# Node numbers of a compare read from PSUM, and two edge tiles instead of one fetched by one-hot products in every second step of the maximum rounds

## The reference: what is computed

```
# L0, one "sum" round: every node sums its neighbours' scaled rows
m_j = norm[:, None] * x[from_]
out = segment_sum(m_j, to_, num_segments=n)

# L3, three "max" rounds (l = 0, 1, 2)
xi = x[dst]
xj = x[src]
h = relu(concat([xi, xj - xi]) @ W1[l] + b1[l])
out = segment_max(h @ W2[l] + b2[l], dst, num_segments=n)
x = relu(where(isfinite(out), out, 0.0))
```

## Time and profile before

| | before |
|---|---|
| median of 3 runs | 8224.27 us (8218.69 to 8224.7) |
| the profiled execution | 8205.95 us, span 8204.1 us |
| busy share | POOL 76%, PE 54%, DVE 47%, PEld 41%, ACT 20% |
| mean granted TensorE clock | 0.686 of full speed |

### The profile page before, as it was taken

One profiled execution on the slowest core, in us unless ns is written; L12 is line 12 of the kernel. 1 busy time (PEld: TensorE's weight loads), 2 busy tenths in 40 slices (PEclk: granted clock), 3 DMA queues, 4 the chain that ended last, 5 costly groups with the idle time before them and its releaser, 6 DMA issues. The chain is left out here.

```text
span 8204.1 us, 96536 instructions
## 1 busy us (share of the span) xinstructions
PE 4466.8 (54%) x27562; PEld 3368.7 (41%) x27562; DVE 3884.1 (47%) x5429; ACT 1605.5 (20%) x2960; POOL 6273.6 (76%) x5477
## 2 busy tenths in 40 slices
PE   2444445665666656621112566666566666666665
PEld 2334334555565555411111344444344444344443
DVE  6555555666646666512212444444444443444444
ACT  0000002333323333300000111121111111111111
POOL 6888886777767777567777788888788887788887
PEclk8667665666656666755555677777677777677776
DMA  7555555777757777622222344443444443444443
GB/s 153 135 134 132 131 129 109 147 147 148 145 116 145 147 146 148 136 72 58 59 58 57 86 96 94 96 95 88 93 95 97 95 95 87 93 96 95 96 96 77
DMA packets 2168031, 886.49 MB, mean 108 GB/s; under 512 B 1794743, under 2 KB 2044260, under 8 KB 2161108
## 3 DMA queue, kind: packets, MB, share of 16 engines
q1 hardware_dynamic: 1083012, 446.95, 23.8%
q10 hardware_dynamic: 909808, 252.48, 13.5%
q0 software_dynamic: 174688, 180.89, 12.0%
HBM read 610.50 MB, written 269.09 MB: 107 GB/s over the span
## 5 line engine op out<-in xcount | busy, mean ns | idle before, releaser
L1183 POOL DMA_INDIRECT edges_a<-src_table,idx x3643 | 4546.7, 1248 | 1265.9 <-issue 1098.8
L1190 POOL DMA_INDIRECT edges_a<-src_table,idx x1616 | 1526.5, 945 | 535.9 <-issue 458.3
L1737 DVE TENSOR_TENSOR early<-src_b,node_id 128x3200 fp8e4<-128x3200 f32 x397 | 1376.7, 3468 | 10.3 <-DMA src_b<-src_rows 10.3
L1757 DVE TENSOR_TENSOR_SCAN st<-pen,st,ps 128x512 f32<-128x512 bf16 x300 | 383.9, 1280 | 1948.2 <-PE ps L1542 1948.2
L1465 PE MATMUL ps<-ident,edges_a 128*128 128x128 f32 x1212 | 482.0, 398 | 1162.2 <-DMA edges_a<-src_table,idx 1161.9
L1455 PE MATMUL ps<-ident,edges_a 128*128 128x128 f32 x808 | 212.2, 414 | 1485.5 <-DVE edges_a L1778 833.9
L1465 PEld LDWEIGHTS ps<-ident,edges_a 128*128 128x128 f32 x1212 | 195.5, 161 | 1430.7 <-DMA edges_a<-src_table,idx 1201.5
L1455 PEld LDWEIGHTS ps<-ident,edges_a 128*128 128x128 f32 x808 | 136.1, 206 | 1550.5 <-DVE edges_a L1778 875.5
L1550 PEld LDWEIGHTS ps<-ident,st 128*128 128x128 f32 (+1 forms) x3636 | 603.0, 190 | 258.6 <-issue 248.1
L1550 PE MATMUL ps<-ident,st 128*128 128x128 f32 (+1 forms) x3636 | 704.9, 334 | 6.1 <-DVE st L1757 6.1
L1468 PE MATMUL ps<-dst_b,win_sb 128*64 128x128 f32 x4848 | 689.5, 374 | 0.0
(11 more groups left out here) (228 smaller groups left out, 5155.7 us busy)
## 6 DMA issues: line engine op xcount, KB each, us to landing
states_sum<-hb ACTq DMA_DIRECT2D x505, 256.0 KB, 3.0
edges_a<-src_table,idx POOLq DMA_INDIRECT x5259
win_sb<-dst_table SPq DMA_DIRECT2D x1616, 48.5 KB
states_att<-hb ACTq DMA_DIRECT2D x202, 388.0 KB
dst_b<-in_dst_row SPq DMA_DIRECT2D x50, 1024.0 KB, 12.0
sel<-onehots SPq DMA_DIRECT2D x305, 128.0 KB, 4.9
win_sb<-dst_table ACTq DMA_DIRECT2D x1212, 32.0 KB
win_sb<-dst_table SPq DMA_DIRECT2D x1212, 32.0 KB
```

The costliest lines, as they stand in the source:

```text
L1183: pool.indirect_dma_start(rows[:, u, j * D:(j + 1) * D], None, srcs[q.r], bass.IndirectOffsetOnAxis(ap=idx[:, h, at:at + 1], axis=0))\
L1190: pool.indirect_dma_start(xe_a[:, s, j * KA:j * KA + D], None, srcs[q.r], bass.IndirectOffsetOnAxis(ap=idx_a[:, s, j:j + 1], axis=0))\
L1737: nc.vector.tensor_tensor(onehot_b[:, i % 2, :, :], src_b[:, h, o:o + P].unsqueeze(1).to_broadcast([P, NB, P]), node_id[:, :].unsqueeze(2) ...
L1757: nc.vector.tensor_tensor_scan(st[0:w, s % V, :], d0, d1, init, op0, op1).then_inc(q.st_ready.sem, 1)
```

## The change

The node numbers are copied once into PSUM (bank 5, `ids_ps`) ahead of the sum round and once ahead of the first max round, and the compare reads them there; its other input stays in SBUF. In the max rounds the pattern of tiles by one-hot products becomes 1, 2, 1, 2 (150 a round), and POOL issues 7, 6, 7, 6 indirect DMAs. All products lie in bank 4 (`pick_ps`), two of them side by side. `picked` and `placed` count steps where they counted tiles, one `place_rows` takes both tiles of a step, and `pick` waits until the step before it has been placed. `src_b` is loaded for two steps at a time, not four.

```
-PICKS = {"sum": (4, (1,)), "max": (1, (1,))}
+PICKS = {"sum": (4, (1,)), "max": (1, (1, 2))}
...
-        last_ids = ps[0:1, 4:6, :].rearrange("p b f -> p (b f)")
+        ids_ps = ps[:, 5, 0:NB]
+        pick_ps = ps[:, 4, 0:2 * PARTS * D]
+        last_ids = ps[0:1, 6:8, :].rearrange("p b f -> p (b f)")
...
+            def step_of(self, i):
+
+                return next((c for c in range(self.first_pick, self.steps) if self.before(c + 1) > i), 0) if i >= 0 else -1
+
+            def picks_up_to(self, c):
+
+                return max(c - self.first_pick + 1, 0)
...
                 def pick(c, s, n):
 
-                    for i in range(q.before(c), q.before(c + 1)):
-                        wait(pe, (q.onehot_made, i + 1), (q.placed, i - 1))
-                        if i == 0:
-                            pe.wait_ge(table_split, q.tables_split)
+                    if not q.picks[c]:
+                        return
+                    if c == q.first_pick:
+                        pe.wait_ge(table_split, q.tables_split)
+                    wait(pe, (q.placed, q.picks_up_to(c - 1)))
+                    for k_, i in enumerate(range(q.before(c), q.before(c + 1))):
+                        wait(pe, (q.onehot_made, i + 1))
+                        at = (1 - k_) * PARTS * D
                         for b in range(NB):
-                            last = nc.tensor.matmul(ps[:, 4 + i % 2, 0:PARTS * D], onehot_b[:, i % 2, b, :],
+                            last = nc.tensor.matmul(pick_ps[:, at:at + PARTS * D], onehot_b[:, i % 2, b, :],
                                                     tables[q.r][:, b, :, :].rearrange("p k f -> p (k f)"),
                                                     start=b == 0, stop=b == NB - 1)
-                        last.then_inc(q.picked.sem, 1)
+                    last.then_inc(q.picked.sem, 1)
...
-                        wait(dve, (q.src_loaded[h], 16 * (use + 1)), (q.picked, i - 1))
+                        wait(dve, (q.src_loaded[h], 16 * (use + 1)), (q.picked, q.picks_up_to(q.step_of(i - 2))))
                         nc.vector.tensor_tensor(onehot_b[:, i % 2, :, :],
                                                 src_b[:, h, o:o + P].unsqueeze(1).to_broadcast([P, NB, P]),
-                                                node_id[:, :].unsqueeze(2).to_broadcast([P, NB, P]), ALU.is_equal,
+                                                ids_ps.unsqueeze(2).to_broadcast([P, NB, P]), ALU.is_equal,
...
-                    for k_, i in enumerate(range(q.before(c), q.before(c + 1))):
-                        j = 2 * TC - 1 - k_
-                        wait(dve, (q.picked, i + 1), (q.turned, c - U + 1))
-                        nc.vector.reduce_sum(rows[:, c % U, j * D:(j + 1) * D],
-                                             ps[:, 4 + i % 2, 0:PARTS * D].rearrange("p (k f) -> p f k", k=PARTS),
-                                             axis=AX.X).then_inc(q.placed.sem, 1)
+                    m = q.picks[c]
+                    if not m:
+                        return
+                    wait(dve, (q.picked, q.picks_up_to(c)), (q.turned, c - U + 1))
+                    nc.vector.reduce_sum(rows[:, c % U, (2 * TC - m) * D:2 * TC * D].rearrange("p (m f) -> p m f", m=m),
...
+                if k in PICKS and (q.r == 0 or ROUNDS[q.r - 1] not in PICKS):
+                    nc.vector.tensor_copy(ids_ps, node_id[:, :]).then_inc(ids_copied, 1)
```

More of the change, by code:

```diff
@@ L272, in gnn_kernel @@
         table_split = sem("table_split")
+        ids_copied = sem("ids_copied")
         LN1, LN2 = ["sum", "mean", "centred", "square", "var"], ["rstd", "norm"]
@@ L388, in __init__ @@
                 if kind in PICKS:
-                    picks, self.span = sum(self.picks), PB // self.most
+                    picks, self.span = sum(p > 0 for p in self.picks), PB // self.most
                     self.src_loaded = [shared(f"src_loaded_{h}", 16 * len(range(self.first_pick + h * self.span, C_,
                                                                                 2 * self.span))) for h in range(2)]
-                    self.onehot_made = shared("onehot_made", picks)
+                    self.onehot_made = shared("onehot_made", sum(self.picks))
                     self.picked = shared("picked", picks)
@@ L1434, in pick @@
                 def pick(c, s, n):
-                    for i in range(q.before(c), q.before(c + 1)):
-                        wait(pe, (q.onehot_made, i + 1), (q.placed, i - 1))
-                        if i == 0:
-                            pe.wait_ge(table_split, q.tables_split)
+                    if not q.picks[c]:
[6 more added lines that the diff above has]
+                        at = (1 - k_) * PARTS * D
                         for b in range(NB):
-                            last = nc.tensor.matmul(ps[:, 4 + i % 2, 0:PARTS * D], onehot_b[:, i % 2, b, :],
+                            last = nc.tensor.matmul(pick_ps[:, at:at + PARTS * D], onehot_b[:, i % 2, b, :],
                                                     tables[q.r][:, b, :, :].rearrange("p k f -> p (k f)"),
                                                     start=b == 0, stop=b == NB - 1)
-                        last.then_inc(q.picked.sem, 1)
+                    last.then_inc(q.picked.sem, 1)
                 def placed(c):
-                    return [(q.placed, q.before(c + 1))] if q.picks[c] else []
+                    return [(q.placed, q.picks_up_to(c))] if q.picks[c] else []
                 def turn(c, s, n):
@@ L1735, in make_onehot @@
                         h, use, o = at % 2, at // 2, (of * q.most + k_) * P
-                        wait(dve, (q.src_loaded[h], 16 * (use + 1)), (q.picked, i - 1))
+                        wait(dve, (q.src_loaded[h], 16 * (use + 1)), (q.picked, q.picks_up_to(q.step_of(i - 2))))
                         nc.vector.tensor_tensor(onehot_b[:, i % 2, :, :],
                                                 src_b[:, h, o:o + P].unsqueeze(1).to_broadcast([P, NB, P]),
-                                                node_id[:, :].unsqueeze(2).to_broadcast([P, NB, P]), ALU.is_equal,
+                                                ids_ps.unsqueeze(2).to_broadcast([P, NB, P]), ALU.is_equal,
                                                 saturate=False).then_inc(q.onehot_made.sem, 1)
                 def place_rows(c, s, n):
-                    for k_, i in enumerate(range(q.before(c), q.before(c + 1))):
-                        j = 2 * TC - 1 - k_
-                        wait(dve, (q.picked, i + 1), (q.turned, c - U + 1))
-                        nc.vector.reduce_sum(rows[:, c % U, j * D:(j + 1) * D],
-                                             ps[:, 4 + i % 2, 0:PARTS * D].rearrange("p (k f) -> p f k", k=PARTS),
-                                             axis=AX.X).then_inc(q.placed.sem, 1)
+                    m = q.picks[c]
[3 more added lines that the diff above has]
+                    nc.vector.reduce_sum(rows[:, c % U, (2 * TC - m) * D:2 * TC * D].rearrange("p (m f) -> p m f", m=m),
+                                         pick_ps[:, (2 - m) * PARTS * D:2 * PARTS * D]
+                                         .rearrange("p (m k f) -> p m f k", m=m, k=PARTS),
+                                         axis=AX.X).then_inc(q.placed.sem, 1)
                 def scan(c, s, d0, d1, op0, op1):
@@ L1869, in _ @@
                     dve.wait_ge(ones_set, 2)
+                if k in PICKS and (q.r == 0 or ROUNDS[q.r - 1] not in PICKS):
+                    nc.vector.tensor_copy(ids_ps, node_id[:, :]).then_inc(ids_copied, 1)
+                    dve.wait_ge(ids_copied, sum(ROUNDS[p] in PICKS and (p == 0 or ROUNDS[p - 1] not in PICKS)
+                                                for p in range(q.r + 1)))
                 if k == ATT:
```

## The result

The changed kernel takes 7054.96 us (median, 7051.56 to 7056.3) against 8221.48 us in the same comparison: ratio 0.8581, 95% interval 0.8566 to 0.8596, 1167 us less. The forecast was 7110 us, within 6950 to 7380.

A forecast was written before the change was run, and what follows sets the result against it. POOL's indirect DMAs were taken as the bound, lengthened by compares holding gathers. Sum round 270 plus three max rounds of 281 gave 1113 us off 8206, so 7093, plus 18 for the median: 7110 us, range 6950 to 7380.

The forecast's parts named there:

- The hold: Compares with two SBUF inputs each hold one POOL gather, 2.7 to 2.9 us on average; with one in PSUM, none.
- The 3.3 us: The most by which one compare was taken to hold a gather, read from a gather of 4.20 us.
- Sum round: Sum round: gather excess of 278 us goes, less under 10 us for small compares; 270 us gained, POOL setting the pace.
- The loop: Max rounds: two steps form one loop through DVE and PE, 16.9 us plus 0.3 for the clock, 17.2 in all.
- the hand sum: Max rounds: compares, placing, picks, hand-overs and scan of two steps added from trace rows and estimates, 16.9 us.
- A max round: Each max round 281 us shorter: 275 from 49.5 step pairs, 6 from held gathers before the first turn.
- Sum: Whole kernel: 270 + 3 x 281 = 1113 us less than the profiled 8206, so 7093.
- the 18 us that I added for the median: Median of the earlier runs lay 18 us above the profiled execution, so 7093 became 7110.
- POOL as the bound: Rival: max-round steps overlap more than thought and POOL stays the bound, gain 1272, 6950 us; chance 0.15.
- The fall of the clock: Rival: PE's clock falls in every max-round step pair, 20 to 21 us a pair, 7600 us; chance 0.15.
- The two rivals about the hold: Something else in the compare holds gathers, 8450 us, chance 0.03; or nothing is held, 8040 us, chance 0.02.
- Loads of `src_b`: Twice as many loads on SP's queue, each asked for two steps (17 us) ahead of its compare, stay hidden.

The follow-up runs named there:

- the filled wait: Changed kernel plus four more PE products in each two-tile step, into the bank that `back` then overwrites: 6986.75 us, ratio 0.8512.
- the kernels with the loop shortened: Changed kernel with PE signalling each product tile, plus either four unneeded PE products per two-tile step (6928.8 us) or DVE's scan one step later (6934.12 us).
- two tiles in every step: Changed kernel with two product tiles in every max-round step instead of 1, 2, leaving 608 gathers a round: 8445.08 us, ratio 1.0284.
- the pattern alone: Changed kernel, but the compare reads the node numbers in SBUF again; pattern 1, 2 and all else kept: 8366.52 us, ratio 1.0186.
- with tiles counted: Changed kernel, but PE signals each product tile, so a one-tile step's compare waits only for the first product before: 7017.62 us, ratio 0.8528.

## Why the prediction was right

- **The hold.** Forecast: it ends entirely, 278 and 272 us of excess a round. In the profile after the gathers take 3325.0 - 3493 x 0.944 = 28 us beyond 0.944 apiece, over all five rounds of the line: 7 in the sum round, 1.3 to 1.4 in each max round, and some 16 in the relation round, whose multiply still reads two tensors in SBUF. That the second SBUF input is the cause is shown by the pair of runs that differ in it alone (7055 and 8367 us). The Trainium skill ("SBUF — State Buffer", Who interferes with whom) states it so, in that an instruction with at most one SBUF input outside the 2-port modes does not contend, and the runs agree; its inference that `tensor_tensor` leaves descriptor generation alone does not carry over to these indirect DMAs, each compare with two SBUF inputs holding one by 2.6 to 2.9 us. No run here separates the reading of their node numbers (`idx`, in SBUF) from the making of descriptors. One reading of the earlier trace rows was off: the held gather ends at 5033.89, 0.83 us behind the compare (5033.06), and not with it. The 3.3 us and the sums don't hang on that.
- **Sum round.** Forecast 270 us less, POOL the bound. The last gather of the round ends at 975.9 us instead of 1245.3, both rounds having begun at 80 to 81 us. There 678 us of gathers and 711 gaps of 0.305 fill the 895 us, so POOL is the bound.
- **The loop.** Forecast 17.2 us for two steps, 16.9 and 0.3 for the clock. Between the second turn and the hundredth a pair took 17.05 us. The two parts were each a little off, and that they nearly cancel is luck. With the clock held (the filled wait) a pair took 16.65, so the hand sum was 0.25 too long: a double product takes 4.30 us and not 4.54, since the second follows faster than the first ran. The clock cost 36 x 1.65 / 147 = 0.40 in these pairs instead of 0.3 (the rows of before gave no size for it).
- **A max round.** Forecast 281 us less. First turn to last was 1137.4 us and is 848.6 (4342.0 to 5190.6), 288.8 less; first gather to first turn was 20.0 us and is 14.5, 5.5 less where I took 6. My 275 for the turns took 22.75 us for a pair of before, the mean over all 100 steps, and 17.2 for one now. Between the second turn and the hundredth a pair was 22.88, so that 49 x (22.88 - 17.05) = 285.7, and the first and the last step together gave the other 3.
- **Sum.** Forecast 1113, in the profiles 8204.1 - 7049.7 = 1154 us: 270 and 3 x 295. The 41 us over are the max rounds' 14 each. The median is 55 us under the forecast: the rest comes from the 18 us that I added for the median, which here lies only 3 us above the profiled execution.
- **The rivals.** POOL as the bound did not come (the kernels with the loop shortened show that it would have been 6930). The fall of the clock came in one pair of four, not in each; two tiles in every step is the case in which the rival would have been right. What I held against it, that the clock fell behind waits of 7 us and more, was a wrong reading: in the earlier trace rows the last turn runs at 0.48 us behind a wait of 4.53, and the granted clock from 5747.20 to 5751.00 is 0.50. So falls behind shorter waits could be seen there already. The two rivals about the hold are ruled out by the pattern alone.
- **Loads of `src_b`.** Hidden, as forecast: DVE waits for them 10.4 us in three places, as before (10.3; one at the start of each max round).

## What to carry to other kernels

Where indirect DMAs issued by POOL sometimes take several times their usual length, look for a DVE instruction that overlaps the long ones and reads two tensors from SBUF; a copy of the smaller one in PSUM costs next to nothing (two copies of 0.19 us) and freed 1097 us here. Once the bound moves to a loop between two engines, fewer instructions on the old bound are worth nothing: write the loop down and look for the wait that counts too much (both products instead of the first). And a PE that waits some 2 us in each turn of such a loop may lose its clock there; a few products into a bank that is about to be overwritten can be cheaper than the idle time.

## What the runs showed of the hardware that I had not expected

The clock fell directly behind waits of 2.06 and 2.14 us, though, as the slow double products tell, only in a part of the cases: behind 36 of the 147 waits of the changed kernel, and, with tiles counted, behind 69 of the 123 waits of 2.06 us. The length of the wait does not decide it by itself, since the shorter wait had the larger share, and equal waits were followed by either. In the changed kernel the slow products came mostly at even distances of 68.2 us, so the moment of the wait seems to count; no run here varies it by itself, and this stays open. With tiles counted the four run times spread by 91 us, in step with their mean clocks, in a kernel whose like agree within 0.3%. Behind waits of 3.66 us (two tiles in every step) the products shown ran at 0.71. Of the 300 double products there, 268 were slow. And some 0.9 us of needless products in the wait, which left 1.25 us of it, brought the clock to 0.99 and, with tiles counted, the spread down to 7 us.
